# A bidirectional state-space block: the skip term moved from a diagonal matmul into the state sum, with other turned and pooled steps

## The reference, cut to what matters

```python
def _mamba(x, ...):                       # once forward, once on the reversed sequence
    u, z = split(x @ in_w.T)              # 256 channels each
    u = silu(conv4(u) + conv_b)
    x_dbl = u @ xproj_w.T                 # dt rank 8, B and C: 16 states each
    dt = softplus(x_dbl[..., :8] @ dt_w.T + dt_b)
    h_t = exp(dt * A) * h_(t-1) + dt * B * u          # 256 channels x 16 states
    y = sum over states of (h_t * C_t)
    y = y + u * D                         # the skip term
    y = y * silu(z)
    return y @ out_w.T
res = x + out_fwd + out_bwd               # then layer norms, a gated feed-forward, layer norms
```

## Time and profile before

| | |
|---|---|
| three runs | 453.68, 457.38, 457.44 us; median 457.38 |
| the profiled execution | 454.6 us, its span 452.8 us |
| mean granted TensorE clock | 0.943 of 2.4 GHz |
| busy: DVE, PE, POOL, ACT | 419.4, 399.6, 396.3, 376.9 us |
| first scan, last scan's end | 22.7 and 424.2 us |

### The profile page before, as it was taken

The page is one execution under the profiler, slowest core; times in us unless marked ns, Lnnn a source line. Parts: engine busy times, 40 slices in busy tenths (PEclk is TensorE's granted clock), DMA queues, the critical chain, the costliest instruction groups (busy, mean ns, idle before and its releaser), DMA issues. The chain is left out here.

```text
span 452.8 us, 6723 instructions
## 1 busy us (share of the span) xinstructions
PE 399.6 (88%) x2273; PEld 271.8 (60%) x2273; DVE 419.4 (93%) x337; ACT 376.9 (83%) x739; POOL 396.3 (88%) x238
## 2 busy tenths in 40 slices
PE   7869967997799899989999799979999986989983
PEld 3446555555566585645756595645756783657963
DVE  4999999899999999999999999989999999998664
ACT  3799998697958999998899999898899899886340
POOL 1688999978999899999989999999979999997531
PEclk9859996997889999999999999989999897999998
DMA  8641222413141213323232323322232313320001
GB/s 240 207 173 64 83 76 81 146 53 118 46 151 59 98 56 122 112 68 117 93 118 69 134 83 112 99 98 71 95 117 98 117 48 116 95 93 1 2 0 46
DMA packets 17633, 42.76 MB, mean 94 GB/s; under 512 B 1600, under 2 KB 7104, under 8 KB 17600
## 3 DMA queue, kind: packets, MB, share of 16 engines
q1 hardware_dynamic: 17600, 42.34, 28.3%
HBM read 40.76 MB, written 1.57 MB: 94 GB/s over the span
## 5 line engine op out<-in xcount | busy, mean ns | idle before, releaser
L1128 POOL TENSOR_TENSOR hq<-hq,c_tiles 128x1024 f32<-128x1024 f32 x127 | 297.8, 2367 | 18.5 <-DVE hq L1281 18.2
L1281 DVE TENSOR_TENSOR_SCAN hq<-da,bb 128x1024 f32<-128x1024 f32 x116 | 262.3, 2279 | 8.2 <-ACT da L914 1.1
L914 ACT ACTIVATE da<-dt,neg_a 128x511 f32<-128x511 f32 x232 | 150.6, 710 | 5.2 <-DVE hq L1281 5.0
L712 PE MATMUL ysum<-wts,hq 128*128 128x128 f32 x1024 | 142.3, 285 | 5.3 <-POOL hq L1128 5.2
L712 PEld LDWEIGHTS ysum<-wts,hq 128*128 128x128 f32 x1024 | 118.4, 146 | 31.1 <-issue 19.9
L1262 DVE TENSOR_TENSOR bb<-bb,dtu 128x1024 f32<-128x1024 f32 x78 | 94.4, 1210 | 3.6 <-PE bb L657 3.0
L1025 ACT ACTIVATE g<-dtu_t,bc_t 128x256 f32<-128x256 f32 x152 | 64.4, 497 | 0.5 <-ACT dtu_t L1013 0.3
L684 PE MATMUL bb<-wts,g 128*128 128x128 f32 x304 | 42.0, 283 | 5.5 <-ACT g L1025 3.0
L684 PEld LDWEIGHTS bb<-wts,g 128*128 128x128 f32 x304 | 35.4, 145 | 14.0 <-issue 8.5
L657 PE MATMUL bb<-b_rows,pick 48*128 48x512 bf16 x74 | 29.7, 401 | 8.9 <-DVE hq L1281 8.9
L657 PEld LDWEIGHTS bb<-b_rows,pick 48*128 48x128 bf16 x74 | 6.9, 93 | 44.2 <-issue 22.7
(11 more groups left out here) (150 smaller groups left out, 495.6 us busy)
## 6 DMA issues: line engine op xcount, KB each, us to landing
c_tiles<-bc_rows_dram SPq DMA_DIRECT2D x64, 512.0 KB, 3.6
b_tiles<-bc_rows_dram SPq DMA_DIRECT2D x12, 256.0 KB, 4.4
x_res<-x_dram SPq DMA_DIRECT2D x1, 768.0 KB, 8.3
out_dram<-o SPq DMA_DIRECT2D x3, 256.0 KB, 2.3
wts<-packed_dram SPq DMA_DIRECT2D x1, 584.0 KB, 9.3
hid<-w_ffn_dram SPq DMA_DIRECT2D x1, 576.0 KB, 7.8
wconv<-conv_taps_dram SPq DMA_DIRECT2D x2, 256.0 KB, 3.8
wconv<-conv_taps_dram SPq DMA_DIRECT2D x1, 512.0 KB, 8.3
```

Source lines behind the costliest of these rows:

```text
L712: mm = nc.tensor.matmul(ysum[:, bank, at], hq[:, i % H_RING, h, block(b)], ident, start=opens, stop=(i % NS == NS - 1), is_transpose=True, ...
L914: ins = nc.scalar.activation(da[:, i % DA_RING, h, 1:SEQ], dt[:, k % 2, h, 1:SEQ], ACT.Exp, scale=neg_a[:, c:c + 1])
L1128: nc.gpsimd.tensor_tensor(hq[:, i % H_RING], hq[:, i % H_RING], c_tiles[:, n % C_RING, i % 2, :].unsqueeze(1).broadcast_to([P, 2, SEQ]), A ...
L1281: nc.vector.tensor_tensor_scan(out=hq[:, i % H_RING].rearrange("p h t -> p (h t)"), data0=decay.rearrange("p h t -> p (h t)"), data1=dbu_t ...
```

## The change

1. `skip_diag` and its matmuls go. In slot 6 of each unit (5 in the last) ACT multiplies `u` by D in place, two activations of 128 x 512 (`u_skip`), and in slot 8 (6 in the last) PE adds it to `ysum` with eight transposes (`skip`). `back` now opens its bank with the transposed `y`.
2. `u` has two buffers instead of three, `g` three instead of two.
3. Turned steps 38 -> 42: unit 1 gets steps 8 and 12, units 2 and 6 step 1. Pooled steps 12 -> 13: unit 0 gets step 8. Plain steps 78 -> 73. In unit 1 the slots of some `g` change.
4. `wo_sum` and `wo_centre` (four activations each) move from slots 8 and 11 of unit 0 to slots 3 and 8 of unit 2, `down_sum` from slot 8 to slot 7 of unit 1.

```diff
-DA_RING, H_RING, BB_RING, C_RING, U_RING = 6, 5, 2, 4, 3
+DA_RING, H_RING, BB_RING, C_RING, U_RING = 6, 5, 2, 4, 2
-G_RING = 2
+G_RING = 3
-TURNED = ((4, 6, 10, 13), (2, 4, 6, 10, 13)) + 2 * ((3, 6, 10, 12, 15), (0, 5, 10, 13)) + (
-    (3, 6, 10, 12, 15), (0, 5, 8, 10, 13, 15))
-POOLED = ((15,), (15,), (8, 14), (15,)) + ((8, 14), (8, 15), (8, 14), (12,))
+TURNED = ((4, 6, 10, 13), (2, 4, 6, 8, 10, 12, 13), (1, 3, 6, 10, 12, 15), (0, 5, 10, 13), (3, 6, 10, 12, 15), (0, 5, 10, 13),
+          (1, 3, 6, 10, 12, 15), (0, 5, 8, 10, 13, 15))
+POOLED = ((8, 15), (15,), (8, 14), (15,)) + ((8, 14), (8, 15), (8, 14), (12,))
...
-             ("turn", 0, 0), ("warm", 3), ("exp_a",), ("skip_diag",), ("u_raw",), ...
+             ("turn", 0, 0), ("warm", 3), ("exp_a",), ("u_raw",), ...
...
+        if k == 1:
+            g_slot = {2: 0, 4: 1, 6: 2, 8: 5, 10: 6, 12: 8, 13: 10}
...
-            put(at + 8, ("neg_mean",), ("wo_sum",))
-            put(at + 11, ("wo_centre",))
+            put(at + 8, ("neg_mean",))
         if k == 1:
-            put(at + 8, ("down_sum",))
+            put(at + 7, ("down_sum",))
             put(at + 11, ("down_centre",))
+        if k == 2:
+            put(at + 3, ("wo_sum",))
+            put(at + 8, ("wo_centre",))
...
         put(z_slot, ("z", k, 0), ("z", k, 1))
         late[z_slot] = z_slot
 
+        put(at + (6 if more else 5), ("u_skip", k))
+        put(at + (8 if more else 6), ("skip", k))
...
+            if 1 in TURNED[n]:
+                put(at + 15, ("g", at + NS + 1))
...
-            if i == STEPS - 1:
-                order += [("skip", UNITS - 1, 0), ("skip", UNITS - 1, 1)]
...
                 elif stage == "skip":
+                    k, = a
+                    pe.wait_ge(s_u_skip, k + 1)
                     for h in range(2):
+                        for b in range(BLK):
+                            bank, at = by_part(h, b) if k == UNITS - 1 else (h, block(b))
+                            mm = nc.tensor.matmul(ysum[:, bank, at], u[:, k % U_RING, h, block(b)], ident,
+                                                  start=False, stop=False, is_transpose=True, skip_group_check=True)
+                    mm.then_inc(s_skip, 1)
...
                 elif stage == "back":
-                    pe.wait_ge(s_diag, 1)
-                    was_read(pe, ("conv_out", k, h))
                     may_write(pe, use)
-                    nc.tensor.matmul(scratch(use), skip_diag[:, d, h, :],
-                                     u[:, k % U_RING, h, ::-1] if d else u[:, k % U_RING, h, :], start=True, stop=False,
-                                     skip_group_check=True)
...
+                elif stage == "u_skip":
+                    k, = a
+                    dtu_ready(act, k)
+                    written(act, ("xproj", k))
+                    for h in range(2):
+                        ins = nc.scalar.activation(u[:, k % U_RING, h, :], u[:, k % U_RING, h, :], ACT.Copy,
+                                                   scale=vec("skip", k % 2, h))
+                    ins.then_inc(s_u_skip, 1)
...
                     if k >= U_RING:
-                        dtu_ready(act, k - U_RING)
-                        written(act, ("gate", k - U_RING, h))
+                        act.wait_ge(s_skip, k - U_RING + 1)
```

More of the change, by code:

```diff
@@ L130, in plan @@
     start = [("ln_stats_in", 0), ("ln_var_first",), ("ln_pow_first",), ("warm", 14), ("normed", 0), ("fold_taps", 0, 0),
-             ("turn", 0, 0), ("warm", 3), ("exp_a",), ("skip_diag",), ("u_raw",), *taps(0, 0), ("neg_a",), ("conv_passes", 0, 1),
+             ("turn", 0, 0), ("warm", 3), ("exp_a",), ("u_raw",), *taps(0, 0), ("neg_a",), ("conv_passes", 0, 1),
              ("fold_taps", 0, 1), ("conv_out", 0, 1), ("conv_out", 0, 0), ("load_softplus",)]
@@ L155, in plan @@
         for p in TURNED[k]:
-            if p:
+            if p >= 2:
                 put(at + g_slot[p], ("g", at + p))
@@ L286, in plan @@
     return order
-PRODUCERS = {"tap": ("conv_out", 3), "xproj_mm": ("xproj", 2), "dt_mm": ("dt", 3), "conv_passes": ("conv_out", 3), "back": ("gate", 3), "skip": ("gate", 3),
+PRODUCERS = {"tap": ("conv_out", 3), "xproj_mm": ("xproj", 2), "dt_mm": ("dt", 3), "conv_passes": ("conv_out", 3), "back": ("gate", 3),
              "oproj_base": ("oproj", 3), "oproj_mm": ("oproj", 3), "oproj_part_mm": ("oproj_part", 1),
@@ L341, in mamba_sandwich @@
         neg_a = sb("neg_a", [P, 4 * NS])
-        skip_diag = sb("skip_diag", [P, 2, 2, P])
         wffn = sb("wffn", [P, 3 * HID])
@@ L421, in mamba_sandwich @@
         s_nega = sem("neg_a_done")
-        s_diag = sem("skip_diagonals_done")
+        s_u_skip = sem("u_scaled_by_skip")
+        s_skip = sem("skip_summed")
         s_full = [sem(f"scratch{n}_written") for n in range(BANKS)]
@@ L716, in _ @@
                 elif stage == "skip":
-                    k, r = a
-                    use, n = ("gate", k, r), HALVES[r][1] - HALVES[r][0]
-                    pe.wait_ge(s_diag, 1)
+                    k, = a
+                    pe.wait_ge(s_u_skip, k + 1)
                     for h in range(2):
-                        was_read(pe, ("conv_out", k, h))
-                    may_write(pe, use)
-                    for h in range(2):
-                        nc.tensor.matmul(scratch(use)[:, h * n * P:(h + 1) * n * P], skip_diag[:, 1, h, :],
-                                         u[:, k % U_RING, h, ::-1][:, cols_of(LAST, r)], start=(h == 0), stop=False,
-                                         skip_group_check=True)
+                        for b in range(BLK):
[3 more added lines that the diff above has]
+                    mm.then_inc(s_skip, 1)
                 elif stage == "back" and a[0] == UNITS - 1:
@@ L730, in _ @@
                     use, (lo, hi) = ("gate", k, r), HALVES[r]
+                    may_write(pe, use)
                     pe.wait_ge(s_yout, 2 * k + turn_of(r) + 1)
@@ L735, in _ @@
                             mm = nc.tensor.matmul(scratch(use)[:, block(2 * h + n)], y_t[:, bank, at], rev,
-                                                  start=False, stop=(h == 1 and n == hi - lo - 1), is_transpose=True,
+                                                  start=(h == 0 and n == 0), stop=(h == 1 and n == hi - lo - 1), is_transpose=True,
                                                   skip_group_check=True)
@@ L753, in _ @@
                         mm = nc.tensor.matmul(scratch(use)[:, block(b)], y_t[:, h, block(BLK - 1 - b if d else b)],
-                                              perm[d], start=False, stop=(b == BLK - 1), is_transpose=True,
+                                              perm[d], start=(b == 0), stop=(b == BLK - 1), is_transpose=True,
                                               skip_group_check=True)
@@ L935, in _ @@
                     nc.scalar.activation(spare[:], col("gamma"), ACT.Silu)
-                elif stage == "skip_diag":
-                    for d in range(2):
-                        for h in range(2):
-                            ins = nc.scalar.activation(skip_diag[:, d, h, :], ident, ACT.Copy,
-                                                       scale=vec("skip", d, h))
-                    ins.then_inc(s_diag, 1)
+                elif stage == "u_skip":
[6 more added lines that the diff above has]
+                    ins.then_inc(s_u_skip, 1)
                 elif stage == "y_out":
@@ L1065, in _ @@
                     act.wait_ge(s_w[1], 16)
+                    act.wait_ge(s_down_sum, 1)
                     for d in range(2):
@@ L1079, in _ @@
                     act.wait_ge(s_wffn, 3)
-                    act.wait_ge(s_wo, 1)
                     for c in range(3):
```

## The result

The change makes the kernel slower: the median of its runs is 475.04 us, and the ratio to the kernel before, run on the same chip, is 1.0323, interval [1.0269, 1.0378]. (Two of the four runs, 477.0 and 477.7, ran at a lower granted clock of 0.907 and are left out of that ratio.) The profiled execution, the shortest of the four, took 468.9 us with a span of 467.0, against 454.6 and 452.8: +14.3 us where the sum said +6.7. The sign was right, the size too small, and the time lies outside the range.

The account below looks back on a forecast made before the run. DVE leads the busy shares, but ACT, late behind `z`, was taken to decide. Terms 3.6 + 0 + 2.2 + 0.5 + 1.1 - 0.7 = +6.7 us on 454.6 give 461.3, taken as 462; range 449 to 467.

Parts of the forecast that it names:

- the sum: Whole kernel: the terms of the units, the end and PE add up to +6.7 us.
- main term: Unit 0: pooled step 8 waits for its `exp_psum` on ACT, so scan 8 starts 3.6 us later; bounds 3.3 to 4.0.
- The stall: Unit 0, ahead of scan 8: DVE stands still for 4.9 us until ACT's `exp_psum` ends.
- the chain to `exp_psum`: Unit 0, ACT behind `z`: `u_skip`, table load, exps of step 11, small copy, `exp_psum`; from 46.74 to 51.8.
- unit 6's saving: Unit 6: turned step 1 saves DVE 1.3 us, kept since PE isn't late there.
- the row: Unit 0, ACT's trace: first exp 1.29 us behind the table load's start, no drain; used instead of the page's extra 1.4 us.
- the part "PE": PE in each unit: two matmuls go (0.9 us of the queue), eight transposes come (0.9); no difference.
- has slack: Unit 3: there is slack for `u_skip` behind `z`, so 0 us.
- slower than the forecast: Rival: unit 0's stall idles PE, half speed fills more of units 1 and 2, 4 to 5 us more: 466; chance 0.10.
- the zero: Unit 1: ACT takes over as the bound, so DVE's 2.6 us saving comes to 0; bounds -2.6 and +0.4.
- the sign of room on ACT: Unit 1: if it lasts under 49.5 us, ACT had room.
- the end: After the last scans: without the old skip matmuls the folds wait for POOL's product of step 126; -0.7 us (-1.9 to 0).

Follow-up runs that it names:

- e3: Kernel before with the changed kernel's step lists, `g` slots and places of `wo_sum` and `down_sum`; skip matmuls and two `g` buffers kept: 459.16 us, 1.0071.
- e4: Changed kernel with `u_skip` moved ahead of `z` (slot 2 of units 1 to 7, slot 12 of unit 0), unit 0's skip transposes in slot 14: 464.71 us, 1.0194.
- e11: Changed kernel with the last unit's skip transposes in slot 12 instead of 6, `u_skip` still in slot 5: 473.43 us, 1.0383.
- e7: e6 plus a thrown-away 512-column matmul in each `back` of units 0 to 6, where the diagonal one stood: 453.68 us, 0.9979.
- e2: Changed kernel with the lists, unit 1 `g` slots and places of `wo_sum` and `down_sum` of before, so the skip alone: 461.64 us, 1.0131.
- e6: e2 with `u_skip` ahead of `z` (slot 2 of units 1 to 7, slot 12 of unit 0): 457.76 us, 1.0031.
- e15: e2 with step 1 of unit 2 turned as the one change to its lists: 465.74 us, 1.0212.
- e14: e2 with step 8 of unit 0 pooled as the one change to its lists: 466.47 us, 1.0231.
- e1: Changed kernel with step 8 of unit 0 plain again: 469.72 us, 1.0324.
- e9: Changed kernel with step 1 of unit 2 plain again: 471.52 us, 1.0354.
- e10: Changed kernel with `wo_sum` and `wo_centre` back in slots 8 and 11 of unit 0: 471.26 us, 1.0349.
- e13: Changed kernel with the old list and `g` slots in unit 1 (steps 8 and 12 plain): 472.21 us, 1.0349.
- e17: Changed kernel with step 1 of unit 2 plain, and `wo_sum` and `wo_centre` back in unit 0: 471.29 us, 1.0345.
- e5: Changed kernel plus a thrown-away 512-column matmul in each `back` of units 0 to 6, where the diagonal one stood: 471.53 us, 1.0365.

## Why the prediction came out as it did

**Unit 0: right in mechanism, and in its main term.** The stall was forecast at 4.9 us and is 4.96; without `u_skip` (e3, e4) it is 3.75, so `u_skip` is 1.2 of it. The unit took 1.4 us more than forecast in this profile: 0.70 for a wait at scan 11 and 0.38 for one at the `mul_b` of step 7, at a clock of 0.78 instead of 0.88; in e11's it took 0.3 less than forecast. (Two slips in the prediction's sums change nothing: the chain to `exp_psum` adds up to 51.7, not 51.8, and unit 6's saving is 1.3 in the text and 1.2 in the sum.) The Trainium skill's page "ScalarE: Activation LUTs", section "What ACT_TABLE_LOAD costs", puts a drain on top of each table load; here the first exp starts 1.29 us behind the load's start again (48.41 to 49.70), so the row held and the drain isn't seen.

**`u_skip`: wrong price, and wrong kind of price.** It was taken at 1.05 us from a Copy out of PSUM; two between SBUF tiles, each scaled by a column, take 1.32 (0.71 each), inside the bounds. That is a mis-sized term of 0.27 us eight times, some 2 us if all of it were in chains. The larger error is that I costed it on ACT's queue alone.

**The step that failed is the part "PE", with its "No difference".** It counted PE's work, 0.9 us out and 0.9 in for each unit. The first of these was itself half of the truth. The trace of before shows what one diagonal matmul takes of the queue (its two records are one matmul), 0.87 us from 189.59 to 190.46:

```profile
189.59 1.02 PE L748 MATMUL scr<-u,skip_diag 128*128 128x512 f32 x2
190.46 0.60 PE L753 MATMUL scr<-wts,y_t 128*128 128x128 f32 x4
```

The filler of e7, of the same shape in the same places, takes the same 0.87 (188.36 to 189.23). Two are 1.7 us, so each unit lost 0.8 us of PE work. Where PE stands waiting, the 1.7 us that went there are only a longer wait. And the step didn't ask what PE, which works in order, waits for now. Waits of 3.79 us (unit 7, `u_skip`) and of 2.09 instead of 0.87 (unit 2, `xdbl`) are PE waits made by ACT's new stage; behind them `bcast` and `g_turn` are late, which DVE feels at once. That is shown by e2 against e6: the same work with `u_skip` ahead of `z` costs 0.3% and not 1.3%, and unit 7 falls from 54.1 to 51.3 us. In units 3 and 5 the place of `u_skip` is the smaller part (0.3 and 0.2 us from e2 to e6); the products that went, with the half speed behind the longer wait, are the larger (1.0 and 1.7 us from e6 to e7). From the two halves of this step together come the misses of +2.5 us in unit 3 (forecast 0, "has slack"), +1.1 in unit 5 and +1.9 in unit 7; the skip alone (e2) has 1.7, 0.7 and 1.9 of them. In unit 6, where I wrote that PE isn't late and the 1.3 us are kept, PE waits 2.0 us for `xdbl` and the unit is 1.2 us longer; even without the skip (e3) it is no shorter than before, so the turned step saved nothing there.

**Half speed had a share of its own, which I gave to a rival.** The rival "slower than the forecast" said that DVE's stall would make PE idle and half speed would fill more of units 1 and 2, once PE is later than DVE in slots 0 to 5. Half speed did grow, from 52 to 69 us. The mechanism is in the traces: PE waits 2.86 us for `xdbl` behind DVE's stall (0.74 before), and half speed begins at 53.4 us, 1 us behind the stall's end. It begins between 53 and 56 us in eight of the ten profiles with step 8 pooled, and in none of the nine others. But it cost little where the rival had put it: units 0 and 1 together have only 3 us more of it (26 to 29), since unit 1, whose clock rose from 0.87 to 0.95, has less. The other 15 us stand in later units, 10.2 of them in unit 3 (from 200.2 us on) and 3.4 more than before in each of units 5 and 7. e6 and e7 show the mechanism with the least between them: the filled wait, the higher clock and the short `xproj` come together. Its price, 466, was 3 us too low even with the mechanism granted.

**Unit 1: the zero can't be judged.** In this profile the unit is 2.2 us shorter, and its 49.2 us are under the 49.5 that the prediction had named as the sign of room on ACT, which took on 3.5 us (46.46 busy of 49.21). In e11's profile the same instructions take 52.4 us, 1.0 more than before; the lists alone (e3) take 51.0. So the zero lies between them, and whether ACT's room is real isn't shown.

**Units 4 and 6, unit 2, the end.** Unit 4 (+0.3 for +0.6) and the end (-0.6 for -0.7) came as worked out. Unit 2 was forecast at +2.2 by an `exp_psum` that is late at step 14; +3.3 came (6.0 in e11's profile), by a `g_turn` that is late at step 12. That the size was near is luck, as the mechanism was another.

**What stays open.** The halves add up to +2.0% and the whole is +3.2%. In us they cost 6.0 and 3.2, 2.5 more than the whole forecast, and some 5.5 come only with both; that is the larger part of what the forecast fell short by, and its cause isn't shown. e15 and e14 put one step of the lists on top of the skip and cost 0.8 and 1.0%, where all the lists without the skip cost 0.7% (the single steps without the skip weren't run); e1, e9, e10, e13 and e17 show that no single item carries it. My guess is that it lies in where half speed falls (its amount alone doesn't do it, by e5), and e15 against e2 shows that it can fall or not behind the same wait of 2.0 us. What decides that, I can't say from these runs. I also don't know whether the interaction would be gone if PE never stood still: that would need a layout of all stages around it, which wasn't tried.

Nothing here beats the kernel before beyond doubt. The best version is e7 with 0.9979 [0.9943, 1.0015], that is, the skip as a sum, `u_skip` ahead of `z`, the old lists, and throwaway products where the diagonals stood: no difference that can be measured, though 3.4% faster than the changed kernel.
